# Folding the odd frequencies of the inverse transform in pairs through one table, with the sine and cosine of the row applied afterwards

## What is computed

```python
U_plus = jnp.fft.irfft(Vf[None, :, :, None] * Uf_p[:, :, None, :], n=n, axis=1)[:, :sl]
U_minus = jnp.fft.irfft(Vf[None, :, :, None] * Uf_m[:, :, None, :], n=n, axis=1)[:, :sl]
...
out = jnp.einsum('btkd,k,kde->bte', U_plus, s, Mpp) + jnp.einsum('btkd,k,kde->bte', U_minus, s, Mpm)
```

## Time and profile before

| | us |
|---|---|
| median of 3 runs | 1842.2 (1836.96 to 1846.12) |
| the profiled execution's own time | 1836.57 |
| its span, first to last instruction | 1835.3 |
| first inverse matmul starts | 1634.16 |
| last instruction of VectorE starts | 1831.88 |

### The profile page before, as it was taken

The page is one execution under the profiler, slowest core; times in us unless marked ns, Lnnn a source line. Parts: engine busy times, 40 slices in busy tenths (PEclk is TensorE's granted clock), DMA queues, the critical chain, the costliest instruction groups (busy, mean ns, idle before and its releaser), DMA issues.

```text
span 1835.3 us, 76477 instructions
## 1 busy us (share of the span) xinstructions
PE 1731.8 (94%) x32475; PEld 1387.5 (76%) x32475; DVE 1312.8 (72%) x3787; ACT 1198.5 (65%) x2619; POOL 637.9 (35%) x815
## 2 busy tenths in 40 slices
...
DMA packets 266001, 182.52 MB, mean 99 GB/s; under 512 B 39888, under 2 KB 263022, under 8 KB 263966
## 3 DMA queue, kind: packets, MB, share of 16 engines
...
...
## 4 chain that ended last, share of the span: by engine, by line
PE 67%; DVE 13%; issue 5%; ACT 4%; POOL 4%; DMA 4%; SPq 3%; DVEq 0%; POOLq 0%; ACTq 0%
PE banks L1401 20%; PE banks L1379 10%; PE banks L1382 9%; PE banks L409 5%; DVE zone L610 4%; PE banks L1601 4%; PE banks L403 3%; SPq L1529 2%; PE banks L368 2%; PE banks L358 2%; PE banks L416 2%; PE banks L382 1%; DMA zone<-Yd 1%; DVE st L597 1%; PE banks L456 1%
## 5 line engine op out<-in xcount | busy, mean ns | idle before, releaser
L1434 DVE COPY Gm<-banks 128x448 f32<-128x448 f32 x896 | 552.8, 639 | 212.5 <-PE banks L1379 126.6
L1420 ACT ACTIVATE Gm<-banks 128x448 f32<-128x448 f32 x896 | 514.9, 628 | 201.2 <-PE banks L1379 151.5
L1401 PE MATMUL banks<-Gm,U 128*32 128x128 f32 x12544 | 515.2, 275 | 13.4 <-issue 6.8
L1401 PEld LDWEIGHTS banks<-Gm,U 128*32 128x32 f32 x12544 | 337.2, 110 | 56.7 <-issue 50.1
L1382 PE MATMUL banks<-V,zone 118*32 118x224 bf16 x7040 | 292.6, 259 | 2.3 <-issue 2.1
L1379 PE MATMUL banks<-V,zone 118*128 118x224 bf16 x1824 | 215.3, 260 | 1.0 <-ACT qT L1206 0.5
L872 POOL TENSOR_TENSOR W<-W,mx 128x280 f32<-128x280 f32 x196 | 130.5, 666 | 227.5 <-DVE mx L659 227.3
L1382 PEld LDWEIGHTS banks<-V,zone 118*32 118x32 bf16 x7040 | 192.8, 96 | 3.8 <-issue 3.1
L1379 PEld LDWEIGHTS banks<-V,zone 118*128 118x128 bf16 x1824 | 156.9, 98 | 47.9 <-issue 40.0
L1601 PE MATMUL banks<-YC,zone 98*98 98x256 f32 x768 | 173.1, 386 | 3.7 <-DVE YC L1673 3.7
L1601 PEld LDWEIGHTS banks<-YC,zone 98*98 98x98 f32 x768 | 129.4, 169 | 52.0 <-issue 8.2
...
## 6 DMA issues: line engine op xcount, KB each, us to landing
Yd<-YS SPq DMA_DIRECT2D x112, 224.0 KB, 4.3
W<-Vd SPq DMA_DIRECT2D x392, 49.0 KB
...
```

What stands on the lines that cost most here:

```text
L1401: ins = e.matmul(p[32 * x:32 * x + 32, :], self.U7[(2 * P + ch) % 3][:, sl, 8 * (3 - q):8 * (3 - q) + 32], self.Gm[:, par, r:r + 2, :], st ...
L1420: e.activation(dst, src, ACT.Copy).then_inc(S["gm_act"], 1)
L1434: v.tensor_copy(dst, src).then_inc(S["gm_dve"], 1)
```

## The change

The odd frequencies are grouped as 4i + 1 and 1 - 4i, so that with sums and differences of each pair ("butterflies") both can be multiplied by tables of the frequency 4i alone, and the output row's angle is applied afterwards as a rotation by its cosine and sine.

- TensorE: "odd" and "mirror" (8 matmuls each) become "straight" and "crossed" (4 each), which read the butterflies in `BF`. The order of a tile becomes two, four, straight, crossed, turn of tile t - 1.
- GpSimd: four butterflies of 98 x (2 x 256) for each pair, and two additions a tile of 98 x 512 (`EO` = `GH` +/- `SP`). GpSimd reads and writes SBUF alone. The first pair's second block is done on VectorE.
- ScalarE: two copies of 98 x 512 a tile from PSUM, scaled by the row's sine (`SP`), two copies of one partition a pair (`fix`), and it issues the stores of a finished pair in place of SyncE.
- VectorE: the two additions to `SC` become two scalar_tensor_tensor, bank times cosine plus `EO`. Its list is put in a new order (`vector`): in iteration t come the whole of tile t - 1, the outer sums of tile t, the turned part of t - 2, the kept part of t - 1, and then at an odd t the odd half of the combine for pair (t // 2) + 2 (`combine_late`), at an even t the even half for pair t // 2 + 1 (`combine_early`). `GH`, `DF` have two buffers each, `EO` and `SC` one.
- SyncE: Y's odd blocks are read with a stride of two rows; the last two odd blocks of pairs 0 and 1 are loaded in two pieces each. The tables are smaller (784 and 1964 columns in place of 3136 twice). Loads for pair n + 2 wait for `combine_early` of pair n; those of RN come behind them.
- In the earlier stages some semaphores are merged (`kzero`, `qbias`, `pset` into `cleared`, `d_sg` into `d_pick`).

The core of the diff; removed lines of `Inverse` are those printed above.

```diff
+                    for a in range(4, 8):
+                        load_y(e, D, D["YL0"], a, 0, 0, 0, (G, G, 70, 70)[a - 4]).then_inc(S["d_yl0"], 16)
                     e.wait_ge(S["sums"], 28 * (Filters.STAGES - 1))
                     e.dma_start(D["rev"], D["c_rev"]).then_inc(S["d_rev"], 16)
-                    for a in range(7):
-                        load_y(e, D, D["YL1"], a, 0, 1).then_inc(S["d_yl1"], 16)
+                    for a in range(8):
+                        load_y(e, D, D["YL1"], a, 0, 1, 0, G if a < 6 else 70).then_inc(S["d_yl1"], 16)
         e.wait_ge(S["d_ylh"], 64)
         e.wait_ge(S["d_y"], 64 * NCH)
-        load_y(e, D, D["YL0"], 7, 0, 0).then_inc(S["d_ylh"], 16)
-        load_y(e, D, D["YL1"], 7, 0, 1).then_inc(S["d_yl1"], 16)
+        for a in range(6, 8):
+            load_y(e, D, D["YL0"], a, 0, 0, 70, G).then_inc(S["d_ylh"], 16)
+        for a in range(6, 8):
+            load_y(e, D, D["YL1"], a, 0, 1, 70, G).then_inc(S["d_yl1"], 16)
         e.wait_ge(S["sums"], 28 * Filters.STAGES)
         load_out(e, D, S, 0)
...
+def load_y(e, D, yl, a, b, pp, p0=0, p1=G):
+    first, step = (G * a, 1) if a < 4 else (392 + 196 * (a // 2 - 2) + a % 2, 2)
+    rows = D["Yd"][first + step * p0:first + step * (p1 - 1) + 1:step]
+    src = rows.rearrange("s (p r b) h x -> s b p r (h x)", r=2, b=4)[:, b, 2 * pp:2 * pp + 2]
+    return e.dma_start(yl[a // 4][p0:p1, 1024 * (a % 4):1024 * (a % 4) + 1024].rearrange("s (p r x) -> s p r x", p=2, r=2), src)
...
+    INVERSE_USES += [("two", _t), ("four", _t), ("straight", _t), ("crossed", _t), ("turn", _t - 1)]
...
+        self.BF = D["BF"]
+        early, late = D["IV"]
+        self.EVT = [t.rearrange("p (a x) -> p a x", a=4) for t in (early, late[:, 0:784])]
+        self.ODT = late[:, 784:1960].rearrange("p (i a x) -> p i a x", i=3, a=2)
+        self.cos, self.sin = late[:, 1960:1962], late[:, 1962:1964]
...
+    def even(self, e, kind, t):
         n, q = t // 2, t % 2
...
+        p, x, lo = self.bank(kind, t), G * q, 2 if kind == "two" else 0
         for c in range(2):
...
+            for a in (lo, lo + 1):
+                ins = e.matmul(p[:, 256 * c:256 * c + 256], self.EVT[c][:, a, x:x + G], self.YC[n % 2][:, c, a],
+                               start=a == lo, stop=a == lo + 1)
+        ins.then_inc(self.S["idft"], 1)
+    def odd(self, e, kind, t, blocks):
+        n, q = t // 2, t % 2
+        p, x, cut = self.bank(kind, t), G * q, t < 2
+        for c in range(2):
+            table, k, s = {("straight", 0): (2, 1, 1), ("straight", 1): (1, 0, 0),
+                           ("crossed", 0): (0, 1, 0), ("crossed", 1): (2, 0, 1)}[kind, c]
+            for a in blocks:
+                ins = e.matmul(p[:, 256 * c:256 * c + 256], self.ODT[:, table, a, x:x + G], self.BF[n % 2][:, k, s, a],
+                               start=a == 0 and (c == 0 or not cut), stop=a == 1 and (c == 1 or not cut))
         return ins
...
+            self.even(e, "two", t)
+            self.even(e, "four", t)
+        e.wait_ge(S["fixed"], 2)
         e.wait_ge(S["ys"], 4 * NCH)
         for t in range(2):
...
+            self.odd(e, "straight", t, (0,))
+            self.odd(e, "crossed", t, (0,))
         e.wait_ge(S["yc"], 3)
         for t in range(2):
...
+            self.odd(e, "straight", t, (1,)).then_inc(S["idft"], 1)
+            self.odd(e, "crossed", t, (1,)).then_inc(S["idft"], 1)
         e.wait_ge(S["d_rev"], 16)
         self.turn(e, 0)
         for t in range(2, 16):
+            n = t // 2
             if t % 2 == 0:
...
+                e.wait_ge(S["yc"], 2 * n + 3)
             self.wait_bank(e, "two", t)
...
+            self.even(e, "two", t)
             self.wait_bank(e, "four", t)
...
+            self.even(e, "four", t)
+            if t % 2 == 0:
+                e.wait_ge(S["fixed"], 2 * n + 2)
+                e.wait_ge(S["bf"], 4 * n + 2)
+            self.wait_bank(e, "straight", t)
+            self.odd(e, "straight", t, (0, 1)).then_inc(S["idft"], 1)
+            self.wait_bank(e, "crossed", t)
+            self.odd(e, "crossed", t, (0, 1)).then_inc(S["idft"], 1)
             self.turn(e, t - 1)
...
         self.turn(e, 15)
     def scalar(self, e):
+        self.keep_half(e, 0)
+        self.keep_half(e, 1)
+        self.fix(e, 0)
         for t in range(16):
...
+            n, q = t // 2, t % 2
             if t >= 2:
...
+                self.keep_half(e, t)
+                e.wait_ge(S["eo"], 2 * (t - 2) + 2)
+            e.wait_ge(S["idft"], INVERSE_DONE["straight", t])
+            e.activation(self.SP[t % 2][:, 0, :], self.bank("straight", t), ACT.Copy, scale=self.sin[:, q:q + 1]).then_inc(S["spun"], 1)
+            e.wait_ge(S["idft"], INVERSE_DONE["crossed", t])
+            e.activation(self.SP[t % 2][:, 1, :], self.bank("crossed", t), ACT.Copy, scale=self.sin[:, q:q + 1]).then_inc(S["spun"], 1)
+            if q == 0 and n + 1 < 8:
+                self.fix(e, n + 1)
+            if q == 1 and n >= 1:
+                e.wait_ge(S["kept"], 4 * n)
+                e.wait_ge(S["turned"], 4 * n)
+                self.store_rows(e, n - 1, slice(0, 4))
...
+    def fix(self, e, n):
+        e.wait_ge(self.S["bf"], 4 * n if n else 2)
+        for s in range(2):
+            e.activation(self.BF[n % 2][0:1, :, s, 0, :], self.YC[n % 2][0:1, :, 4 + s].rearrange("p k q x -> p k (q x)"),
+                         ACT.Copy).then_inc(self.S["fixed"], 1)
...
+    def combine_early(self, v, n):
+        S = self.S
+        if n == 0:
+            v.wait_ge(S["d_ylh"], 64)
+            v.wait_ge(S["sums"], 28 * (Filters.STAGES - 1))
+        elif n >= 2:
+            v.wait_ge(S["idft"], INVERSE_DONE["four", 2 * n - 3])
+        self.combine(v, n, 0, 0)
+        self.combine(v, n, 0, 1).then_inc(S["yc"], 1)
+    def combine_late(self, v, n):
+        S = self.S
+        v.wait_ge(S[f"d_yl{n % 2}"], (64 if n % 2 == 0 else 160) + 128 * (n // 2))
+        if n >= 2:
+            v.wait_ge(S["bf"], 4 * (n - 2) + 4 if n > 2 else 2)
+            v.wait_ge(S["fixed"], 2 * (n - 2) + 2)
+        self.combine(v, n, 1, 0)
+        self.combine(v, n, 1, 1).then_inc(S["yc"], 1)
+    def butterfly(self, e, n, a, s):
+        yc, bf = self.YC[n % 2].rearrange("p k a q x -> p k a (q x)"), self.BF[n % 2]
+        plus, minus = yc[:, :, 4 + 2 * a], yc[:, :, 5 + 2 * a]
+        if s == 0:
+            return e.tensor_tensor(bf[:, :, 0, a, :], plus, minus, ALU.add)
+        return e.tensor_tensor(bf[:, :, 1, a, :], minus, plus, ALU.subtract)
+    def first_blocks(self, v):
+        S = self.S
+        v.wait_ge(S["d_yl0"], 64)
+        self.combine(v, 0, 1, 0, 0, 2)
+        self.combine(v, 0, 1, 1, 0, 2).then_inc(S["yc"], 1)
+        v.wait_ge(S["d_ylh"], 96)
+        self.steps.tick(self.combine(v, 0, 1, 0, 2, 4))
+        self.steps.tick(self.combine(v, 0, 1, 1, 2, 4))
+        v.wait_ge(self.steps.sem, self.steps.n)
+        v.wait_ge(S["gmm"], 32 * (Filters.STAGES - 2))
+        self.steps.tick(self.butterfly(v, 0, 1, 0))
+        self.butterfly(v, 0, 1, 1).then_inc(S["yc"], 1)
+    def outer(self, v, t):
+        S, ch = self.S, self.steps
+        pb, pa, gh = self.PB[t % 2], self.bank("four", t), self.GH[t % 2]
+        v.wait_ge(S["half"], t + 1)
+        v.wait_ge(S["idft"], INVERSE_DONE["four", t])
+        if t >= 2:
+            v.wait_ge(S["eo"], 2 * (t - 2) + 2)
+        v.tensor_tensor(gh[:, 0, :], pa, pb[:, :], ALU.add).then_inc(S["gh"], 1)
+        v.tensor_tensor(gh[:, 1, :], pa, pb[:, :], ALU.subtract).then_inc(S["gh"], 1)
+    def whole(self, v, t):
+        S, ch, q = self.S, self.steps, t % 2
+        sc = self.SC.rearrange("p a c x -> p a (c x)")
+        v.wait_ge(S["spun"], 2 * t + 2)
+        for a, kind in ((1, "crossed"), (0, "straight")):
+            v.wait_ge(S["eo"], 2 * t + 2 - a)
+            v.scalar_tensor_tensor(sc[:, a], self.bank(kind, t), self.cos[:, q:q + 1], self.EO[:, a], ALU.mult, ALU.add
+                                   ).then_inc(S["rows"], 1)
+        v.wait_ge(S["rows"], 2 * t + 2)
+        if t >= 2:
+            v.wait_ge(S["tmm"], t - 1)
+        v.tensor_tensor(self.DF[t % 2][:, :, :], self.SC[:, :, 0, :], self.SC[:, :, 1, :], ALU.subtract).then_inc(S["tdif"], 1)
+        ch.tick(v.tensor_tensor(self.NT[:, :, :], self.SC[:, :, 0, :], self.SC[:, :, 1, :], ALU.add))
...
     def vector(self, v):
+        self.combine_early(v, 0)
+        self.first_blocks(v)
+        self.outer(v, 0)
+        self.combine_late(v, 1)
+        self.outer(v, 1)
+        self.combine_early(v, 1)
+        for t in range(1, 18):
+            if t <= 16:
+                self.whole(v, t - 1)
+            if 2 <= t < 16:
+                self.outer(v, t)
+            if t >= 2:
+                self.turned(v, t - 2)
+            if t <= 16:
+                self.kept(v, t - 1)
+            if t < 14:
+                n = t // 2 + 1
+                if t % 2:
+                    self.combine_late(v, n + 1) if n + 1 < 8 else None
```

(75 more changed lines are left out.)

163 lines of the change are left out of this document (38 added, 125 removed).

## The result

The changed kernel takes 1826.9 us (median of 4 runs, 1826.2 to 1827.8), the kernel before 1840.6 in the same session: ratio 0.9926, 95% interval 0.9904 to 0.9948. That is 2.2 us under the forecast of 1829.0. The profiled execution took 1826.17 us, its span is 1824.9 (1835.3 before). One slow execution of the kernel before, 3350 us in the first session of the experiments, is in no ratio here.

What follows compares the result with a forecast made beforehand. VectorE and GpSimd taking turns at SBUF were to set 21.8 us a pair: start to 1684.5, five pairs to 1793.5, end 28.5, span 1822.0; 13.3 us off the median gives 1829, range 1807 to 1846.

Steps and rivals of the forecast that it cites:

- Layout of an iteration: Steady state, VectorE and GpSimd laid out together: odd iteration 9.1 us, even 12.7, a pair 21.8 against 24.1 before.
- The turns: VectorE instructions with two SBUF inputs and GpSimd additions wait for each other; 1024 VectorE elements cost GpSimd about 1.0 us.
- the rule of the Trainium skill: Exclusive SBUF lock when VectorE has two SBUF inputs and GpSimd reads; said to forbid moving these additions to GpSimd.
- The new form, SC, and GpSimd's addition: VectorE's scalar_tensor_tensor priced like L1711 (683 ns), SC, SC, DF, NT 2.62 us together; a GpSimd addition 1.25 us.
- Start: Inverse stage's beginning: first odd blocks at 1652, pair 1's butterflies 1655.6 to 1662.5, first even iteration ends 1684.5.
- Tail: After pair 7's early combine, tiles 14 and 15 remain, at a low clock first: 28.5 us against 43.1 before.
- The sum: Span 1793.5 + 28.5 = 1822.0 us, 13.3 under 1835.3; taken off the median 1842.2, this gives 1829.
- TensorE: Inverse-stage matmuls: 55 us less work, 15.6 us a pair; idles in most iterations at a lowered clock, just hidden.
- the clock rival: TensorE stays at 1.2 GHz: 31 us a pair, median 1886; chance 0.1, shared with other slower causes.
- Transfers: Loads and stores of a pair take 20.3 us, hidden under the 21.8 us pair by 1.5 us only.
- the lock costs little: Rival: waits fall where engines idle anyway, transfers set the pace at 20.3 us a pair; median 1814, chance 0.2.
- Where the gain comes from: Whole inverse stage: the end gives back what the start and the five pairs hardly bring; 13.3 us in all.

Runs made afterwards that it cites:

- e1: Changed kernel with GpSimd's inverse-stage instructions from tile 1 on cut from 512 to 8 columns, the rest left out: 1795.0 us, ratio 0.9728.
- e8: Changed kernel with each GpSimd addition of the inverse stage from pair 1 on replaced by two memsets: 1798.7 us, ratio 0.9756.
- e4: Changed kernel with GpSimd's butterflies held back by waits to run beside VectorE work with a PSUM input, nothing left out: 1808.4 us, ratio 0.9809.
- e6: Changed kernel with the odd blocks' matmuls of tiles 2 to 15 issued twice, back to 48 records a tile: 1841.5 us, ratio 0.9985.

## Why the prediction was right

The time, 1829.0 for 1826.9, came out by the mechanism that was forecast. Its terms:

- **Layout of an iteration.** Offsets from SC, forecast and measured: EO starts 3.9 and 4.0, ends 6.6 and 6.7; odd iteration 9.1 and 9.15; in the even one NT ends 3.6 and 3.7, EO 7.6 and 7.8, the whole 12.7 and 12.89. The pair: 21.8 and 22.04. The turns read from two pairs of rows carried this (e1 and e8 show the cause for the instructions with two SBUF inputs). VectorE's waits for EO, 3.9 us in all, lie at the start (2.45 and 0.40) and in the tail, so GpSimd isn't the bound. The prediction's sentence that the rule of the Trainium skill (SBUF — State Buffer, Who interferes with whom) would forbid moving these additions says more than the rule does: it says which overlaps block, and e4 shows that a placed addition costs nothing.
- **The new form, SC, and GpSimd's addition.** SC, SC, DF, NT take 2.64 us (1707.27 to 1709.91) where 2.62 was taken, an addition on GpSimd 1.26 where 1.25 was. The reason given for the first, that L1720 at half the size is mostly fixed cost, was wrong: 481 ns at 256 and 737 ns at 512 elements leave some 225 that don't grow. The two SC take 1.43 us from start to start where they took 1.31; this was small enough not to matter.
- **Start.** First odd blocks ready, both butterflies included, 1653.2 (forecast 1652), the butterflies of pair 1 from 1656.8 to 1663.9 (1655.6 to 1662.5), first even iteration ended 1685.25 (1684.5), pair 7's early combine 1795.42 (1793.5).
- **Tail.** 29.5 us (28.5). Low clock behind the wait for DF, as forecast: 16 records in 4.78 us (5.6), with a turn of 1.64 (1.8). What was taken too low is the end: the last turn ran at low clock too, 2.00 us where 1.0 was taken, and from the end of VectorE's last instruction (1821.8) to the span's end it is 3.1 us where 2.5 was.
- **The size was met in part by luck.** The sum gave a span of 1822.0 and it was 1824.9, 2.9 over. The median came out 2.2 under the forecast, because the profiled execution of the changed kernel lay 0.7 us below its median, and that of the kernel before 5.6 below the median the forecast started from. The two misses have opposite signs.
- **TensorE.** Idle in front of most turns, clock 0.84 to 0.92 over a pair, and hidden, as forecast; the clock rival (1886) has no support in any run.
- **Transfers: wrong.** I took 20.3 us a pair from the earlier trace rows as a limit. It was none: e1 moved the same bytes in 16.6. Why the kernel before was slower with them is not shown. Its DMA engines were not waiting for requests: from 1681 to 1693 they were busy for 0.95 to 0.98 of the time at 254 to 278 GB/s, and in e1, as busy, they moved 258 to 337. The rival "the lock costs little" would have ended near e1's 1795 and not at 1814, and the low end of the range was too high for it. The forecast didn't rest on this term; e4's did, and was too cautious.
- **Where the gain comes from.** Right: the end gives what start and pairs together don't bring. Five pairs take 110.2 us where they took 120.4, but the start, up to the end of pair 2's early combine, takes 34.6 (1650.63 to 1685.25) where it took 21.9; in sum the body is 2.5 longer. e6 gives TensorE 48 of its 55 us back and is 11 us slower by the ratios, 13.7 in the stage, nearly all in the tail: one tile less behind the last combine and two shorter ones. In the body TensorE's 22.4 us a pair were exchanged for the 22.04 of VectorE and GpSimd. Of the 2.04 us by which a pair became shorter, 1.65 are there in e6 as well, so they don't come from the smaller work of TensorE.

Still open, and it is where these 1.65 us lie: why the kernel before waits 1.7 us a pair for Y at a DMA share of 0.75 and 0.76 over a pair, and e6, with the same TensorE load, doesn't. The strided loads, the order of issues and the stores' other queue all differ, and none was tried alone.
